# Local convolution input by block transposes on VectorE instead of a padded image in DRAM

## What is computed

```
x = x + L0(gn(x))     3x3 convolution, batch norm, ReLU, then a curvature from small periodic filters
x = x + L1(gn(x))     a 3x3 convolution whose taps are mixed by a per-pixel operator (tanh)
x = x + L2(gn(x))     gn(x) * (1 + sigmoid(gate_w * |sobel(blur difference of the gray image)| + gate_b))
x = x + L3(gn(x))     global(gn(x)) * local(gn(x))
```

## Time and profile before

| what | value |
|---|---|
| runs | 4078.0 us median of 3 (4065.13 to 4078.7) |
| the profiled execution's own time | 4077.41 us |
| its span, first to last instruction | 4075.6 us |
| mean granted TensorE clock | 0.908 of full speed |
| tails, from `tail_sum` of image 0 to the end of `conv3` | about 3166 to 3758 us of the span |
| mixing of modes and the way of its result over DRAM | about 3758 to 3860 us |
| output loop | from about 3860 us |

### The profile page before, as it was taken

One profiled execution on the slowest core, in us unless ns is written; L12 is line 12 of the kernel. 1 busy time (PEld: TensorE's weight loads), 2 busy tenths in 40 slices (PEclk: granted clock), 3 DMA queues, 4 the chain that ended last, 5 costly groups with the idle time before them and its releaser, 6 DMA issues.

```text
span 4075.6 us, 90045 instructions
## 1 busy us (share of the span) xinstructions
PE 3379.0 (83%) x32900; PEld 1222.0 (30%) x32900; DVE 2816.1 (69%) x3537; ACT 1849.0 (45%) x2702; POOL 2199.2 (54%) x1035
## 2 busy tenths in 40 slices
PE   4669999479999999999999999999998368876444
PEld 2334444112222222222222222222221346554433
DVE  3643455379989899899899899899997454540034
ACT  0115555445555555555555455555553455552010
POOL 0000000079999999999999999999997000000000
PEclk9889999789999999999999999999999678787555
DMA  6574887656666666656666566666664589877487
GB/s 159 119 171 95 183 173 164 153 140 153 154 141 145 144 147 153 149 138 147 143 154 150 139 147 144 154 148 147 148 149 107 123 185 211 189 166 155 102 208 207
DMA packets 530804, 621.89 MB, mean 153 GB/s; under 512 B 73266, under 2 KB 369330, under 8 KB 524011
## 3 DMA queue, kind: packets, MB, share of 16 engines
q1 hardware_dynamic: 519812, 599.07, 64.6%
q10 hardware_dynamic: 10560, 16.93, 1.7%
HBM read 428.02 MB, written 201.84 MB: 155 GB/s over the span
## 4 chain that ended last, share of the span: by engine, by line
PE 30%; issue 28%; POOL 28%; DMA 4%; ACT 4%; DVE 3%; SPq 2%; ACTq 0%; POOLq 0%; DVEq 0%
POOL arena L1138 26%; PE ps L607 7%; PE ps L566 7%; PE ps L614 4%; PE ps L678 3%; DMA arena<-l_dram 2%; ACT arena L897 2%; PE ps L764 2%; POOL arena L1126 2%; PE ps L786 2%; PE ps L859 1%; PE ps L660 1%; DVE arena L1491 1%; PE ps L835 1%; SPq L511 1%
## 5 line engine op out<-in xcount | busy, mean ns | idle before, releaser
L1423 DVE TENSOR_TENSOR arena<-ps,arena 128x1024 f32<-128x1024 f32 x1792 | 2106.4, 1219 | 206.7 <-PE ps L660 175.2
L1138 POOL TENSOR_TENSOR arena<-arena 128x1024 f32<-128x1024 f32 x896 | 1931.5, 2201 | 555.6 <-ACT arena L1000 555.5
L678 PE MATMUL ps<-arena,w_mix 128*32 128x512 f32 x10752 | 1439.1, 607 | 79.3 <-POOL arena L1138 79.3
L1000 ACT ACTIVATE arena<-ps 128x1024 f32<-128x1024 f32 x896 | 918.1, 1025 | 1028.1 <-PE ps L670 1017.0
L660 PE MATMUL ps<-arena,sel 48*128 48x512 bf16 x3584 | 702.3, 385 | 25.3 <-issue 16.5
L660 PEld LDWEIGHTS ps<-arena,sel 48*128 48x128 bf16 x3584 | 190.3, 93 | 945.9 <-issue 937.4
L566 PE MATMUL ps<-arena,w_conv 32*32 32x512 f32 x9216 | 374.1, 682 | 94.2 <-issue 74.9
L670 PE MATMUL ps<-norms,opw 57*128 57x512 bf16 x1792 | 348.5, 384 | 49.2 <-ACT arena L932 17.6
L678 PEld LDWEIGHTS ps<-arena,w_mix 128*32 128x32 f32 x10752 | 214.4, 108 | 468.1 <-issue 468.1
L897 ACT ACTIVATE arena<-arena,nmr,rstd 128x128 f32<-128x128 f32 x768 | 301.1, 482 | 12.0 <-DVE nmr L1182 12.0
L607 PE MATMUL ps<-arena,circ 128*128 128x512 f32 x640 | 287.9, 595 | 14.0 <-ACT arena L911 14.0
(11 more groups left out here) (148 smaller groups left out, 2100.0 us busy)
## 6 DMA issues: line engine op xcount, KB each, us to landing
arena<-pad SPq DMA_DIRECT2D x768, 260.0 KB, 7.7
split_dram<-arena SPq DMA_DIRECT2D x64, 768.0 KB, 3.6
arena<-split_dram SPq DMA_DIRECT2D x1536, 32.0 KB, 3.2
pad<-arena SPq DMA_DIRECT2D x16, 2080.0 KB, 15.4
x_dram<-arena SPq DMA_DIRECT2D x16, 2048.0 KB, 10.2
l_dram<-arena SPq DMA_DIRECT2D x128, 256.0 KB, 4.7
arena<-x_dram SPq DMA_DIRECT2D x16, 2048.0 KB, 14.3
arena<-l_dram SPq DMA_DIRECT2D x32, 1024.0 KB, 18.4
```

Of the source, the lines that this page charges most:

```text
L678: m = pe.matmul(ps[C * g:C * g + C, SUM + chunk % 2, :], w_mix[:, s, :], ring[:, (first + g // 2) % size, NPX * (g % 2):NPX * (g % 2) + NP ...
L1000: nc.scalar.activation(ring_p[:, slot, :], ps[:, POOL_BANK:POOL_BANK + 2, :].rearrange("p a n -> p (a n)"), ACT.Tanh).then_inc(tanh_p, 1)
L1138: nc.gpsimd.tensor_tensor(slot, slot, pixels(chunk % 2, SPREAD[n // 2], n % 2), ALU.mult).then_inc(prod_p, 1)
L1423: nc.vector.tensor_tensor(slot, weights, pixels(par, ONCE[n // 2], n % 2), ALU.mult).then_inc(prod_d, 1)
```

## The change

`pad3` goes, with its stores, loads, border constants and semaphores. In its place VectorE transposes 32x32 blocks straight from `xn3` to `cpad`, for each column of the image one block per group of 32 partitions: row 32 g + r of channel c goes to partition 32 g + c, band row r + 1. Two small transposes fill the wrap columns. Then GpSimd copies, for each of the four bands, its first and last row from the neighbouring bands (partitions of another group of 32). `conv3` waits for `halo_ready`, set by GpSimd. On SP the second half of `bands_out` moves behind the store of the residual stream, and the wait for `gn3.out` now stands ahead of `tail_in`.

```diff
@@ SP, borders
-                for pad in (pad1, pad3):
-                    sp.dma_start(pad.ap()[b:b + 1, C * PLANE:PADDED], gray[0:1, 0:TAIL]).then_inc(border_done, 16)
+                sp.dma_start(pad1.ap()[b:b + 1, C * PLANE:PADDED], gray[0:1, 0:TAIL]).then_inc(border_done, 16)
@@ SP, tails
             for t in range(B):
                 par = t % 2
                 if t >= 2:
-                    bands_out(t - 2)
+                    bands_out(t - 2, 0)
                 sp.wait_ge(x3_done, 4 * (t + 1))
                 sp.dma_start(x3_dram[t], xd[par]).then_inc(x3_stored[par], 16)
-                sp.wait_ge(gn3.out, 4 * (t + 1))
-                sp.wait_ge(wrap_ready, t + 1)
-                rows = image_rows(pad3, t)
-                sp.dma_start(rows[1:H + 1], xn3[par]).then_inc(xn3_stored[par], 16)
-                sp.dma_start(rows[0:1], xn3[par][H - 1:H, :, :]).then_inc(xn3_stored[par], 16)
-                sp.dma_start(rows[H + 1:H + 2], xn3[par][0:1, :, :]).then_inc(xn3_stored[par], 16)
+                if t >= 2:
+                    bands_out(t - 2, 1)
                 if t + 2 < B:
+                    sp.wait_ge(gn3.out, 4 * (t + 1))
                     sp.wait_ge(x3_stored[par], 16 * (t // 2 + 1))
                     tail_in(t + 2)
-                sp.wait_ge(xn3_stored[par], 48 * (t // 2 + 1))
-                after(sp, conv3_mm, 2 * (t - 1))
-                bands = bass.AP(tensor=pad3, offset=t * PADDED, ap=[[PLANE, C], [RB * PW, G], [1, XSPAN]])
-                for g in range(G):
-                    sp.dma_start(cpad[par][C * g:C * g + C, :, :].rearrange("p r w -> p (r w)"), bands[:, g, :]).then_inc(cpad_loaded[par], 16)
@@ PE, conv3
-                    pe.wait_ge(cpad_loaded[t % 2], 64 * (t // 2 + 1))
+                    pe.wait_ge(halo_ready, t + 1)
@@ ACT, tails
-                    after(act, xn3_stored[t % 2], 48 * (t // 2))
+                    after(act, bands_ready, t - 1)
@@ POOL, after layer 1
+            for t in range(B):
+                tile = cpad[t % 2]
+                pool.wait_ge(bands_ready, t + 1)
+                for g in range(G):
+                    above, own, below = (slice(C * (n % G), C * (n % G) + C) for n in (g - 1, g, g + 1))
+                    nc.gpsimd.tensor_copy(tile[own, 0, :], tile[above, RB, :])
+                    m = nc.gpsimd.tensor_copy(tile[own, XROWS - 1, :], tile[below, 1, :])
+                m.then_inc(halo_ready, 1)
@@ DVE, tails
+            def bands(i):
+
+                rows = xn3[i % 2].rearrange("p c w -> p w c")
+                out_ = cpad[i % 2][:, 1:RB + 1, :].rearrange("p r w -> p w r")
+                after(dve, conv3_mm, 2 * (i - 1))
+                dve.wait_ge(gn3.out, 4 * (i + 1))
+                nc.vector.transpose(out_[:, 1:W + 1, :], rows[:, 1:W + 1, :])
+                nc.vector.transpose(out_[:, 0:1, :], rows[:, W:W + 1, :])
+                nc.vector.transpose(out_[:, PW - 1:PW, :], rows[:, 1:2, :]).then_inc(bands_ready, 1)
+
@@ DVE, tails, loop over i
                 if i + 1 < B:
                     tail_sum(i + 1)
-                dve.wait_ge(gn3.out, 4 * (i + 1))
-                tile = xn3[i % 2]
-                nc.vector.tensor_copy(tile[:, :, 0:1], tile[:, :, W:W + 1])
-                nc.vector.tensor_copy(tile[:, :, PW - 1:PW], tile[:, :, 1:2]).then_inc(wrap_ready, 1)
+                bands(i)
```

More of the change, by code:

```diff
@@ L107, in four_layers @@
     pad1 = dram("pad1", (B, PADDED))
-    pad3 = dram("pad3", (B, PADDED))
     parts_dram = dram("parts_dram", (B, 3 * PLANE + TAIL), BF16)
@@ L280, in four_layers @@
             "rows_mm", "rows_tanh", "rows_diag", "rows_h", "rows_r", "rows_m", "rows_l"))
-        xd_loaded, ld_loaded, x3_stored, xn3_stored, cpad_loaded, l3_stored = (two(n) for n in (
-            "xd_loaded", "ld_loaded", "x3_stored", "xn3_stored", "cpad_loaded", "l3_stored"))
+        xd_loaded, ld_loaded, x3_stored, l3_stored = (two(n) for n in (
+            "xd_loaded", "ld_loaded", "x3_stored", "l3_stored"))
         x2_done, gray_mm, gray_done, dog_mm, dog_copy, sob_mm, sob_sq, mag_sum, mag_root, att_tanh, gain_done, att_mul, x3_done = (once(n) for n in (
             "x2_done", "gray_mm", "gray_done", "dog_mm", "dog_copy", "sob_mm", "sob_sq", "mag_sum", "mag_root", "att_tanh", "gain_done", "att_mul", "x3_done"))
-        wrap_ready, dfth_mm, dfth_copy, dftw_mm, dftw_copy, conv3_mm, conv3_evac = (once(n) for n in (
-            "wrap_ready", "dfth_mm", "dfth_copy", "dftw_mm", "dftw_copy", "conv3_mm", "conv3_evac"))
+        bands_ready, halo_ready, dfth_mm, dfth_copy, dftw_mm, dftw_copy, conv3_mm, conv3_evac = (once(n) for n in (
+            "bands_ready", "halo_ready", "dfth_mm", "dfth_copy", "dftw_mm", "dftw_copy", "conv3_mm", "conv3_evac"))
         wm_loaded, spec_mm, spec_copy, spec_stored, spec_loaded = (once(n) for n in ("wm_loaded", "spec_mm", "spec_copy", "spec_stored", "spec_loaded"))
@@ L300, in four_layers @@
         PARS = 10
-        BORDERS = (2 * (2 + 1) + 3) * B
+        BORDERS = (2 * (2 + 1) + 2) * B
         HALF = CHUNKS // 2
@@ L476, in _, with bands_out @@
             tail_in(1)
-            def bands_out(t):
+            def bands_out(t, half):
                 bands = l3_dram[t].rearrange("c (g e j r) w -> e j c g (r w)", g=G, e=HALVES, j=4)
[L481 to L484, removed]
+                sp.wait_ge(conv3_evac, 2 * t + half + 1)
+                for j in range(4):
+                    sp.dma_start(bands[half, j], lo3[C * j:C * j + C, half, :, :]).then_inc(l3_stored[half], 16)
             for t in range(B):
@@ L514, in _ @@
             for t in (B - 2, B - 1):
-                bands_out(t)
+                for half in range(HALVES):
+                    bands_out(t, half)
             sp.wait_ge(spec_copy, 8)
```

1 line of the change is left out of this document (removed).

## The result

The changed kernel takes 4099.4 us (median of 5, 4096.5 to 4100.6) against 4076.6 (5 runs): ratio 1.0059, interval 1.0045 to 1.0072. Run again beside the experiments on one chip it took 4098.9 against 4069.6, ratio 1.0070 (1.0056 to 1.0084). It is slower by 0.6 to 0.7%. 4115 had been forecast, with a range of 4074 to 4150. The profiled execution took 4096.5, its span is 4094.7, 19.1 us longer than before.

The account below looks back on a forecast made before the run. In the tails a latency chain through the joint of two images was taken as the bound, with no engine full. 51.1 + 1.3 - 8.9 - 6 = +37.5 us on 4077.4 gave 4115 us, range 4074 to 4150.

Parts of the forecast that it names:

- The 51.1: Joints of images 0 to 6: VectorE's added transposes lie on the latency chain, 7 x 7.3 us.
- the cover of 1.6: Images 3 and 6: the next means waited for TensorE anyway, 1.25 and 0.35 us, which takes off 1.6.
- 7.3 us added an image: VectorE in the tails: big transpose 7.1 us at the channel sum's rate, plus 0.2 for the two small ones.
- the add's rate: VectorE's two-operand add, 1.03 ns an element; at that rate the transpose's 4096 elements take 4.4 us.
- rival B: VectorE's transpose streams at the add's rate whatever the step: 4.6 us an image, 4096 us; chance 0.22.
- 8.9 us for the evacuation: Stage end: ScalarE's evacuation of image 7's first half waits for TensorE alone, no longer a DMA; 8.9 us gained.
- GpSimd's copies, bounded at 17.6 us: Tails: 8 copies of 32 partitions x 130, at most 2.2 us each, ready before the last convolution.
- The bounds are 0 and 13; I credit 6: TensorE's unexplained gaps, about 13 us on the chain: less DMA traffic shortens them, 6 us credited.
- the slow first DFT rows: Images 3 and 6: TensorE's first 32 DFT matmuls slow to 6.88 us as elsewhere, adding 0.9 + 2.0 = 2.9.
- The count there: TensorE's unexplained gaps on the chain in the last stretch, counted as 4.17 us.
- A: Main forecast: transposes at the channel sum's rate on the chain, +37.5 us, 4115 us; chance 0.50.
- Rival D: All TensorE gaps go (-13), transposes cost 2.4 + 0.2 us: 4075 us; decides under 2.9 us an image; chance 0.15.

Follow-up runs that it names:

- experiment 1: Changed kernel with each image's transposes moved behind the next image's gn2 scale (image 7's stay): 4023.9 us against 4069.1 for the kernel before, ratio 0.9893.
- experiment 11: Changed kernel with the big transpose in four forms, contiguous or stepped, two images each, plus five single operations; single run, read for durations alone.
- experiment 7: Kernel before the change with only image 6's first band stores issued ahead of the spectral weight loads: 4062.2 us against 4069.1, ratio 0.9979.
- experiment 8: Changed kernel with image 7's padded-image stores and loads put back behind the weight loads: ratio 1.0106 against the kernel before.
- the late version: The kernel of experiment 1, transposes behind the next image's gn2 scale: 4023.9 us; with the padded image's stores and loads put back 4031.4 us.
- experiment 2: Kernel before the change with its two wrap copies and their gn3 wait moved behind the next image's gn2 scale: 4064.9 us against 4069.6, ratio 0.9991.
- experiment 10: Kernel before the change with only the second half of the band stores issued behind the store of the residual stream: ratio 1.0017.
- experiment 9: Changed kernel with the weight loads held until image 7's transposes are done, behind image 6's first band stores: ratio 1.0070 against the kernel before.

## Why the prediction was right, point by point

- **The place.** That the transposes lie on the chain at full price, since VectorE's list has them ahead of the next image's means, held in each of the 7 joints and is shown by experiment 1, which moved them (and their wait, worth 1.2 us a joint) and nothing else. The 51.1 less the cover of 1.6, 49.5, came out as 52.1.
- **The price.** 7.3 us added an image was 7.8. The nearest row, the channel sum, had the right size. The choice between it and the add's rate decides the sign of the result: with the 4.45 us of the contiguous form the measured +19.1 would be some -5, an estimate from 7 x 3.41. The reason given for the write was wrong in general: "Writing with such a step costs nothing by itself" comes from a memset of 32 elements; a transpose that steps its write alone costs 7.86 us as well. It did no harm, since the steps do not add up. The Trainium skill's rule on new lines for each element, SBUF — State Buffer, "Door 1: The DMA port swizzle", agrees in direction with experiment 11 (1.22 against 2.10 us). The one element per cycle that the Trainium skill gives the transposing array in Vector Engine (DVE) Microarchitecture Reference, section 3.8, was forecast to lead to rival B; a rate like B's came only in the contiguous form, 4.45 us. Rival B's transpose fell with that.
- **The end of the stage.** 8.9 us for the evacuation that no longer waits for a store: 9.8 in experiment 7. GpSimd's copies, bounded at 17.6 us, took 2.6.
- **The gaps of TensorE: the mis-sized term.** "The bounds are 0 and 13; I credit 6." Gaps that "grow or vanish" stood among the signs of being wrong, and ahead of the convolution they vanished. With the slow first DFT rows taken out as forecast (+2.9; 49.5 us for 46.6), the stretches and the end shrank by 28.4 + 2.9 - 9.8 = 21.5 us more than order explains: 10.2 in the loop and 11.3 at the end. That is 15.5 of the 18.4 us between the 37.5 forecast and the 19.1 of the span; the scatter outside the tails (-4.6) and the order of stores (-0.9) go the same way, the joints (+2.6) the other.

  At the end the cause is shown, since experiment 8 brings 7.7 of the 11.3 back. The count there had one gap of two; the other stood ahead of the convolution's second half and is 0.72 us after the change:

```profile
3700.01 0.50 PE L776 MATMUL ps<-k,arena 128*32 128x32 f32 x18 [4.30 <-issue]
```

  Around its own gap the convolution also ran slower, 18.6 us for 288 matmuls and a gap at a granted clock of 0.78 before, 10.4 at 1.00 after. In the loop no run brings the 10.2 back: with the traffic in it the changed kernel's stretches stay at 327.5 us. Up to 5 of the 10.2 may be scatter, and the rest stays open.
- **The number.** 4099.4 lies nearer to rival B's 4096 than to the 4115 of A. The mechanism is A's, and the distance is made up of the terms just named; that B's number came close is chance, for its transpose was 3.2 us too cheap an image and its gap credit as low as A's.
- **Rival D** had it right that the gaps go, though only a part of them was shown to be the traffic's, and the transpose wrong: at 7.86 us the transposes are far over the 2.9 from which it would have decided.

## What to carry to other kernels

Before an operation is put on an engine, look in that engine's list for what stands behind it: the same 8 us of transposes cost 55 us or nothing, depending on whether the next image's statistics stood behind them, and the idle stretch that hides them began 3 us behind that `mu` (3536.78 and 3539.68 in experiment 1). Where no row shows an operation, take the row that shares its access pattern, not the one that shares its arithmetic, and ask of both sides of the pattern. DMA that nobody waits for can still have a price in a full stage, and putting the traffic back without its use is a cheap way of reading it; it showed here that the price (7.7 us at the end, 7.5 in the late version, nothing in the changed kernel's loop) hangs on whether TensorE has time to spare.

## What was not expected of the hardware

- A step of 520 B on one side of an f32 operation of VectorE nearly halves its rate, and a second stepped side costs next to nothing more: transpose 4.45 us contiguous, 7.87 with a stepped write, 7.85 with a stepped read, 7.86 with both; copy 2.29 contiguous, 4.11 with a stepped read, 4.20 with both.
- TensorE's unexplained gaps follow the padded image's stores and loads (0, 9.9, 11.2, 23.0 us for none, stores, loads, both), yet 4 MB of weight loads at a DMA share of 0.87 to 1.25 made none in the one stretch tried. The gaps keep to places in TensorE's program: in the last stretch one stands ahead of the last 50 of the 288 matmuls in the kernel before (4.17 us), in experiments 2 (4.49), 7 (4.17), 8 (3.13) and 10 (4.49), and elsewhere they are often 128 matmuls apart. That speaks for something tied to its instructions. Whether TensorE's instructions wait behind these transfers, and what distinguishes the weights' transfers (size of piece, direction, what had been fetched before), stays open: no run separated it.
- 288 convolution matmuls without a gap took 9.8 to 10.6 us at a granted clock of 1.00 (2.4 GHz) and 11.3 us at 0.85. Halves that begin behind a 2.3 us wait for an evacuation came out both ways: 9.81 us at 1.00 in experiment 9, 11.35 at 0.85 in the changed kernel.
